# Where four small steps of a fused RWKV-6 and feed-forward kernel stand: block copy, differences, gate scaling and a load

## The reference, cut to what matters

```python
xx = x_prev - x                                   # x_prev: the token before
mix = tanh((x + xx * time_maa_x) @ maa_w1) ...    # five low-rank mixings
r, k, v = xr @ Wr.T, xk @ Wk.T, xv @ Wv.T
g = silu(xg @ Wg.T)
decay = exp(-exp(time_decay + tanh(xw @ td_w1) @ td_w2))
y_t = r_t (S + u * k_t v_t);  S = decay_t * S + k_t v_t      # 16 heads of 32
y = ((y - mean) / sqrt(var + EPS)) * ln_g + ln_b  # per head
x = layernorm(x + (y * g) @ Wo.T)
h = layernorm(gelu(x @ absmean(W_fc).T)) ;  x = layernorm(x + h @ absmean(W_proj).T)
```

## Time and profile before

| | us |
|---|---|
| median of 3 runs | 3052.81 |
| lowest, highest | 3050.32, 3054.34 |
| profiled execution, its own time | 3053.38 |
| span of its instructions | 3051.6 |

### The profile page before, as it was taken

One profiled execution on the slowest core, in us unless ns is written; L12 is line 12 of the kernel. 1 busy time (PEld: TensorE's weight loads), 2 busy tenths in 40 slices (PEclk: granted clock), 3 DMA queues, 4 the chain that ended last, 5 costly groups with the idle time before them and its releaser, 6 DMA issues.

```text
span 3051.6 us, 101627 instructions
## 1 busy us (share of the span) xinstructions
PE 2890.4 (95%) x40249; PEld 2119.1 (69%) x40249; DVE 2488.5 (82%) x5437; ACT 1927.5 (63%) x4079; POOL 934.2 (31%) x790
## 2 busy tenths in 40 slices
PE   3899999999999999999999999999999999999997
PEld 2576767777767777767777767777767777767775
DVE  6778888878888878888778888778888778888777
ACT  1466666666666666666666666666667666667664
POOL 3223332233332233332233332233332233332232
PEclk8899999999999999999999999999999999999999
DMA  6000000000000000000000000000000000000000
GB/s 217 15 16 16 23 12 23 19 23 16 23 12 23 19 23 16 23 12 23 19 23 16 23 12 23 19 23 16 23 13 23 19 23 16 23 13 23 19 23 15
DMA packets 22523, 73.40 MB, mean 24 GB/s; under 512 B 2805, under 2 KB 3061, under 8 KB 20469
## 3 DMA queue, kind: packets, MB, share of 16 engines
q1 hardware_dynamic: 22132, 67.10, 6.6%
HBM read 50.31 MB, written 16.78 MB: 22 GB/s over the span
## 4 chain that ended last, share of the span: by engine, by line
PE 65%; DVE 21%; issue 9%; ACT 2%; SPq 1%; DMA 1%; DVEq 1%; ACTq 0%; POOLq 0%; POOL 0%
PE psP L408 18%; PE psF L661 11%; PE psP L634 7%; PE psP L450 7%; PE psF L680 4%; DVE HLO L1394 4%; PE psY L532 2%; DVE ARENA L1267 2%; PE psY L548 2%; DVE SUMS L1386 2%; DVE ARENA L1131 2%; DVE ARENA L1205 1%; DVE ARENA L1331 1%; PE psW L489 1%; DVE ARENA L1119 1%
## 5 line engine op out<-in xcount | busy, mean ns | idle before, releaser
L408 PE MATMUL psP<-ARENA,WALL 128*128 128x256 f32 x3072 | 698.6, 382 | 4.9 <-ACT ARENA L752 2.7
L710 ACT ACTIVATE ARENA<-ARENA 32x512 f32<-32x512 f32 (+3 forms) x930 | 523.8, 563 | 201.2 <-DVE ARENA L1205 96.1
L408 PEld LDWEIGHTS psP<-ARENA,WALL 128*128 128x128 f32 x3072 | 577.7, 191 | 83.3 <-POOL ARENA L933 4.2
L1394 DVE SCALAR_TENSOR_TENSOR HLO<-GG,FWB,HHI 128x128 f16<-128x128 f32 x1024 | 347.6, 400 | 283.5 <-ACT HHI L882 278.5
L661 PE MATMUL psF<-XHI,WFC 128*128 128x128 f16 x4096 | 487.9, 220 | 2.2 <-DVE ST L1410 1.9
L661 PE MATMUL psF<-XLO,WFC 128*128 128x128 f16 x4096 | 486.3, 219 | 0.0
L916 POOL TENSOR_TENSOR MT<-ARENA 32x256 fp32r<-32x256 f32 x330 | 319.2, 967 | 439.7 <-ACT ARENA L710 411.0
L933 POOL TENSOR_TENSOR ARENA<-ARENA,XT 128x1024 f32<-128x1024 f32 x128 | 279.5, 2183 | 512.7 <-DVE ARENA L1131 512.7
L661 PEld LDWEIGHTS psF<-XHI,WFC 128*128 128x128 f16 x4096 | 397.8, 98 | 41.0 <-issue 32.9
L661 PEld LDWEIGHTS psF<-XLO,WFC 128*128 128x128 f16 x4096 | 401.8, 98 | 17.6 <-issue 10.3
L680 PE MATMUL psF<-WPJ,HHI 128*128 128x512 f16 x1024 | 389.6, 380 | 13.8 <-ACT GG L873 13.8
(11 more groups left out here) (166 smaller groups left out, 5226.8 us busy)
## 6 DMA issues: line engine op xcount, KB each, us to landing
XT<-x_ch SPq DMA_DIRECT2D x33, 520.0 KB, 3.4
ARENA<-x_tok SPq DMA_DIRECT2D x32, 512.0 KB, 5.0
out<-OUT SPq DMA_DIRECT2D x64, 256.0 KB, 2.1
WALL<-w_all SPq DMA_DIRECT2D x5, 1024.0 KB, 16.5
ARENA<-wfc SPq DMA_DIRECT2D x4, 1024.0 KB, 8.0
ARENA<-wpj SPq DMA_DIRECT2D x3, 1024.0 KB, 25.5
GG<-wpj SPq DMA_DIRECT2D x1, 1024.0 KB, 24.4
OUT<-w2a SPq DMA_DIRECT2D x2, 256.0 KB
```

The lines of the kernel that those rows point to most:

```text
L408: mm = pe.matmul(psP[:, P.bank(f"{name}{g}"), COLS * c:COLS * (c + 1)], WALL[:, w, k, 128 * (2 * g + c):128 * (2 * g + c + 1)], cc(XF[slot ...
L710: return act.activation(o, i, ACT.Copy)
L1394: e = dve.scalar_tensor_tensor(out=HLO[:, k, :], in0=GG[:, u % 2, 0, 128 * m:128 * (m + 1)], scalar=FWB[:, 0, k:k + 1], in1=HHI[:, k, :], ...
```

## The change

Four edits, all in the last third of a tile.

1. GpSimd's block copy (L960) now comes ahead of the scale root `finish` (L926). Its `settled` wait asks only for the roots of the tile before.
2. On VectorE, `finish` and `outputs(1)` come ahead of `differences(it + 1)`, and `up(1, 0)` ahead of `normed`.
3. The scaling of the gate G by ln_b goes from VectorE (four instructions of 128x256 per tile, L1318) to GpSimd (one of 128x1024, behind the output's root, after a wait for `y_weighed`).
4. SP starts the token-wise load after `values(1)` ("kv1") instead of after the second transposition of keys ("kt1").

```diff
@@ block.sync, tile
-                sp.wait_ge(x_full, X.full(it, "kt1"))
+                sp.wait_ge(x_full, X.full(it, "kv1"))
                 sp.dma_start(XTOK[:, :, :], x_tok[it]).then_inc(xtok_in, 16)
@@ block.gpsimd, tile
                 if ffn:
                     ffn.bias()
-                    ffn.finish()
...
                 pool.wait_ge(ab_rest, it + 1)
+                if ffn:
+                    ffn.finish()
                 pool.wait_ge(tot_ready, NPL * it + 6)
...
                 if ffn:
                     ffn.normed()
+                pool.wait_ge(y_weighed, it + 1)
+                pool.tensor_tensor(G.rearrange("p (c t) -> p c t", c=KC), G.rearrange("p (c t) -> p c t", c=KC),
+                                   PAR[:, :, LN_B:LN_B + 1].broadcast_to([128, KC, COLS]), ALU.mult).then_inc(y_affine, 1)
 
                 pool.wait_ge(s_decayed, it + 1)
+                pool.wait_ge(y_affine, it + 1)
...
                 def settled():
                     pool.wait_ge(x1_biased, PAIRS * (j + 1))
-                    pool.wait_ge(root_taken, 2 * PAIRS * j + 1)
+                    pool.wait_ge(root_taken, 2 * PAIRS * j)
@@ block.vector, tile
                 if ffn:
                     ffn.stats()
+                if ffn:
+                    ffn.finish()
+                outputs(1)
                 dve.wait_ge(m_dve, M.read(it, "mg1"))
                 differences(it + 1)
                 if ffn:
-                    ffn.finish()
-                outputs(1)
-                if ffn:
+                    ffn.up(1, 0)
                     ffn.normed()
-                if ffn:
-                    ffn.up(1, 0)
...
-                dve.wait_ge(y_weighed, it + 1)
-                for k in range(KC):
-                    dve.tensor_scalar(cc(G, k), cc(G, k), PAR[:, k, LN_B:LN_B + 1], None, ALU.mult).then_inc(y_affine, 1)
...
-                    dve.wait_ge(y_affine, KC * it + 4)
+                    dve.wait_ge(y_affine, it + 1)
```

## The result

The changed kernel takes 3065.53 us (median of five runs, 3062.80 to 3067.53), the kernel before 3051.16 us (median of five, 3050.32 to 3054.34). The ratio is 1.0045, with an interval of 1.0034 to 1.0055: **slower by about half of what was forecast**. The time lies inside the range and on the forecast side, but where +0.85 us a tile was predicted, a tile got longer by 0.42 us. That number is the mean distance from one `outputs(0)` to the next over 21 tiles in the middle of each trace: 91.62 us before, 92.03 after. The profiled execution shown here took 3067.53 us.

What follows compares the result with a forecast made beforehand. It took TensorE's work plus its few waits as the bound, a tile changing as the end of `mixed_by_x` moves: 31 x 0.85 = 26.4 us on top of the kernel before gave 3079.5 us, range 3060 to 3098.

Steps and rivals of the forecast that it cites:

- The stall: TensorE's wait for GpSimd's block copy before `from_chunk(1)` (L548), once in each of 31 tiles: all 1.34 us would go.
- The meeting with the decay: VectorE's `differences`, now behind `outputs(1)`, held by GpSimd's state decay (L968) until 1599.32; next step at 1600.33 instead of 1599.97.
- The half-price rival: The decay doesn't hold `differences`; all is 0.36 us earlier up to the scaling, +0.49 a tile, 3068 us; chance 0.08.
- The gate scaling: One 128x1024 instruction on GpSimd, taken as 2.18 us, from 1604.17 to 1606.35, starting half a microsecond before `mixed_by_x`.
- The hold on `mixed_by_x`: GpSimd's scaling holds VectorE's first L1119, which ends 0.28 us after it; `mixed_by_x` ends at 1607.83 against 1606.98, +0.85 us.
- the start-up row: In the start-up, two `mixed_by_x` instructions take 1.65 us beside GpSimd's L902 and end 0.27 us after it.
- The leading faster rival: GpSimd's scaling doesn't hold VectorE; `mixed_by_x` ends 0.64 us earlier a tile, 3033.5 us; chance 0.12 with its faster variants.
- The new waits: TensorE's tanh argument (L368) waits for `mixed_by_x` until 1607.9, through at 1610.4, before Gelu frees L680's bank near 1610.8.
- The load: Token-wise load waits for `values(1)`, lands at 1608.3, 11 us before its reader L1343: costs nothing.
- The worse one: The output's root (L926, 0.55 to 0.63 us) gets in front of `weighed` on VectorE: +1.40 a tile, 3096.5 us; chance 0.07.
- The 0.04 for no change: Rival with chance 0.04: the gained stall and the held steps cancel, as with a scaling shorter by about 0.85 us.

Runs made afterwards that it cites:

- copy and load: The kernel before with only GpSimd's block copy ahead of the root and the token-wise load begun after `values(1)`: 3021.60 us, ratio 0.9891, period 90.59.
- copy, `finish` first, load later: The kernel before with the block copy ahead of the root, VectorE's `finish` ahead of `differences` ahead of `outputs(1)`, and the load after `values(1)`: 3007.23 us, ratio 0.9844.

## Why the forecast came out as it did

**The stall.** Right. "The stall of 1.34 us goes whole": L548 starts 1.42 us earlier (1604.26 - 7.26 = 1597.00 against 1598.42), and `outputs(1)` 1.41 earlier. The term was 0.07 too small, because 1.34 is the idle time that was shown and the first matmul of a group that doesn't wait also overlaps the one before it. The root beside no `differences` took 0.55 us (0.63 was said).

**The meeting with the decay.** Right, to 0.1 us. `differences` is 1.57 us long, not 1.23, and ends at 1600.33 (forecast 1600.41). `weighed` starts 0.07 later than before although all ahead of it began 1.41 earlier. The half-price rival is out. What the order costs is seen against copy and load: 90.88 - 90.59 = 0.29 us a tile without the scaling.

**The gate scaling. This is the step that failed**, by its size: "Its nearest row is L933 ... 2.18 us. The lower bound is two of L968's size (2 x 1.05); I take 2.18." It took 1.90, less than both ends. The upper row was of another kind than I said: L933 reads two operands of full size, while the scaling repeats a few values along the second one, as L968 does. And the lower bound counted a fixed part twice. From L968 and the scaling itself, 512 more elements cost 1.90 - 1.05 = 0.85 us, so that 1.05 - 0.85 = 0.20 is fixed. One instruction of twice the size is cheaper than two. A bound by 2 x 1.05 was an upper bound, not a lower one. With the full operand the same instruction took 2.36 us, more than L933's 2.18. The 0.28 of 2.18 - 1.90 and the 0.08 by which the scaling began early account for 0.85 - 0.48 = 0.37 in the shown tile (the rows sum to within 0.01). In the mean over 21 tiles the increase is 0.42.

**The hold on `mixed_by_x`.** Right: the first L1124 lasts 1.68 us and ends 0.28 after the scaling (1611.85 + 1.68 = 1613.53 against 1613.25), as worked out from the start-up row. The leading faster rival, that the scaling doesn't hold VectorE, gave -0.64 a tile. The kernel with the scaling put back comes in at 90.88 - 91.62 = -0.74, so that rival priced the way without a hold well; but the hold is there. The Trainium skill, page "SBUF — State Buffer", section "Who interferes with whom", says that the other engine "fully blocks", and that held for `mixed_by_x` in every kernel with the scaling on GpSimd: the doubled and the lengthened scaling were paid at 1.65 for 1.96 and 0.46 for 0.46. One pair of before doesn't fit a simple order of starts: L1402 (two operands in SBUF) starts 0.29 us after a root on GpSimd and yet takes its usual 0.68 us.

One reading of the forecast was wrong, without harm to the sum. It takes VectorE's instructions with one operand as not touched, and calls L1355 a case of the rule for two operands in SBUF. L1355 reads one operand, and it lasts 0.86 us beside L933 in 31 tiles and 0.17 in the one tile without it. The diagonal copy behind `outputs(0)` has one operand too, and the block copy now runs beside it. Before, after, and a state addition with one of two operands in PSUM, beside the scaling:

```profile
1593.84 0.42 DVE L1222 COPY ARENA<-ARENA 32x512 f32<-32x512 f32 x1
...
1601.10 0.84 DVE L1227 COPY ARENA<-ARENA 32x512 f32<-32x512 f32 x1
...
1611.52 0.41 DVE L1293 TENSOR_TENSOR ARENA<-ARENA,psY 128x256 f32<-128x256 f32 x1
```

The copy is held for 0.42 us in every tile, where some 0.3 was said; it comes out of VectorE's idle time before `outputs(1)`, as said. The addition isn't held.

**The new waits.** L368 starts at 1607.60 on the old scale, after 1.67 us of idle (1607.9 was said). L680 starts at 1610.43 with an idle time of 0.26, as before: it wasn't made later than the Gelu allows.

**The load.** "It costs nothing" is right for the change and for the load alone (1.0003). The working behind it was not complete. I looked at the load's reader only, and not at what else uses the queues while it runs: with the stall gone, the early load costs 0.31 to 0.88 us a tile.

**The rivals of the sum.** The worse one, the output's root in front of `weighed`, didn't occur. The 0.04 for no change named the very failure ("as when the scaling is shorter by about 0.85"), but at three times its size.

## What to carry to other kernels

Price an instruction with a fixed part and a part by element from two sizes of the same kind of operands: half-size rows added up are not a lower bound. Work that is moved to GpSimd off a chain costs what VectorE's steps beside it lose. Held here were steps with two operands in SBUF, and of those with one a copy and a `tensor_scalar` between SBUF tiles; not held were those that read one of two operands from PSUM, and `BATCH_NORM_STATS2`. So move it beside steps that the trace shows as not held, and put such steps as `differences` where GpSimd has nothing long. And when a stall is removed, look for what it covered: here a product on VectorE and a large load, and only with both out of the way (copy, `finish` first, load later; the scaling left on VectorE) did the whole stall of 1.4 us a tile become time, 3007 us.

## What the runs showed of the hardware

- A data load of 512 KB and one instruction transfer of 0.02 MB at the same time: with the load begun early, the transfer came 4.2 us after `outputs(0)`, with the load begun late, 2.1 us, and TensorE stood for 0.94 us in the middle of a matmul group in the first case and not in the second. Tile by tile, in three kernels with the early load, each of the 42 tiles with a late transfer has that idle and none of the 21 with an early one. The Trainium skill, page "SBUF — State Buffer", section "Who interferes with whom", says that DMA never contends with a compute engine. For operands nothing here speaks against that; the load kept TensorE idle all the same, by the reading above by way of the instructions.
- TensorE's clock after idle time: after 3.31 us without work 14 of 21 tiles ran L368 slowly, after 2.12 us eight, after 1.67 us none. In the tile shown, 4 us had a granted clock of 0.57, and L368 took 3.42 us instead of 1.99. In the mean the waits of 3.31 and 2.12 us cost 0.8 and 0.4 us a tile on top of themselves.
- The hold works in both directions. A 128x1 root on GpSimd took 1.60 us beside `differences` and 0.55 without it; a decay of 128x512 took 1.05 us and made the `differences` beside it 0.34 us longer.
- It isn't confined to VectorE's steps with two operands: a copy of 32x512 between SBUF tiles took 0.84 us beside GpSimd's block copy instead of 0.42, and a `tensor_scalar` of 128x2 took 0.86 beside L933 instead of 0.17, though one of 128x1 (L1439) kept its 0.15 there. A `tensor_tensor` of 128x256 with one operand in PSUM took 0.41 beside the scaling, and `BATCH_NORM_STATS2` 0.68 beside the decay, as without them.
